# First attention of a two-layer decoder kernel: roots ahead of the weight blocks, weights cast one pair sooner

## The reference

```python
x = x + _L0_xattn_ref(_layernorm(x), ctx_1024, ctx_1024, mask)     # first attention, 16 batches
x = x + _L0_ffn_ref(_layernorm(x), ...)                            # 4 experts, 2 chosen for each batch by a gate
x = x + _L1_xattn_ref(_layernorm(x), ctx_1024, ctx_1024, ...)      # causal attention with 16 heads
x = x + _L1_ffn_ref(_layernorm(x), ...)                            # shared and chosen experts
```

## Time and profile before

| | us |
|---|---|
| median of 3 runs | 785.7 (784.28 to 785.91) |
| the profiled execution | 787.21 |
| its span | 785.4 |
| VectorE busy in the span | 621.0 |
| TensorE busy in the span | 717.4 |
| the gate's last products end | 90.4 after the start of the span |

### The profile page before, as it was taken

One profiled execution on the slowest core, in us unless ns is written; L12 is line 12 of the kernel. 1 busy time (PEld: TensorE's weight loads), 2 busy tenths in 40 slices (PEclk: granted clock), 3 DMA queues, 4 the chain that ended last, 5 costly groups with the idle time before them and its releaser, 6 DMA issues.

```text
span 785.4 us, 29153 instructions
## 1 busy us (share of the span) xinstructions
PE 717.4 (91%) x11006; PEld 571.9 (73%) x11006; DVE 621.0 (79%) x1803; ACT 337.8 (43%) x711; POOL 381.0 (49%) x647
## 2 busy tenths in 40 slices
PE   5688759999999999999999999999989999997896
PEld 5566547888888888888888888888766666665684
DVE  4777655788888887978787878788889988997864
ACT  4665423434343434343434344443455555553310
POOL 1788833354454445453535353544434544546354
PEclk9886689999999999999999999999999999999798
DMA  8776600000000000000000000000122222322120
GB/s 289 235 235 221 208 1 3 3 3 3 3 3 3 3 3 3 3 3 3 3 3 3 3 4 3 3 10 16 35 64 69 88 83 83 115 89 69 34 76 7
DMA packets 24655, 40.98 MB, mean 52 GB/s; under 512 B 3855, under 2 KB 16793, under 8 KB 24267
## 3 DMA queue, kind: packets, MB, share of 16 engines
q1 hardware_dynamic: 23096, 37.13, 14.4%
q0 software_dynamic: 704, 1.71, 0.8%
q10 hardware_dynamic: 726, 0.30, 0.2%
HBM read 30.60 MB, written 8.91 MB: 50 GB/s over the span
## 4 chain that ended last, share of the span: by engine, by line
PE 70%; DVE 15%; issue 5%; POOL 5%; ACT 4%; DMA 0%; POOLq 0%; ACTq 0%; DVEq 0%
PE ps L490 7%; PE ps L484 7%; PE ps L492 6%; PE ps L491 6%; PE ps L687 6%; DVE mx L1499 5%; PE ps L629 4%; PE ps L705 4%; PE ps L743 4%; PE ps L745 4%; PE ps L744 3%; PE ps L631 3%; PE ps L630 2%; PE ps L741 2%; PE ps L621 2%
## 5 line engine op out<-in xcount | busy, mean ns | idle before, releaser
L1113 ACT ACTIVATE pT<-ps 128x1024 f32<-128x1024 f32 x96 | 93.1, 1021 | 123.7 <-PE ps L687 123.7
L1499 DVE TENSOR_REDUCE mx<-ps 128x16 f32<-128x2048 f32 x48 | 109.5, 2281 | 1.0 <-PE ps L648 1.0
L2049 POOL TENSOR_TENSOR y<-y,vec 128x256 f32<-128x256 f32 x32 | 23.2, 724 | 170.7 <-DVE y L1270 170.7
L743 PE MATMUL ps<-xh,w_hi 128*128 128x128 bf16 x512 | 99.4, 219 | 0.0
L744 PE MATMUL ps<-xl,w_hi 128*128 128x128 bf16 x512 | 99.3, 219 | 0.0
L745 PE MATMUL ps<-xh,w_lo 128*128 128x128 bf16 x512 | 99.2, 219 | 0.0
L1959 POOL TENSOR_TENSOR rs<-rs,cst 128x1 f32<-128x1 f32 x132 | 75.6, 573 | 10.3
L1957 POOL TENSOR_TENSOR rs<-mv,cst 128x1 f32<-128x1 f32 x132 | 29.7, 225 | 102.2 <-DVE mv L1267 96.1
L490 PE MATMUL ps<-w_hi,hh 128*128 x256 | 69.8, 273 | 0.0
L491 PE MATMUL ps<-w_hi,hl 128*128 x256 | 69.8, 273 | 0.0
L492 PE MATMUL ps<-w_lo,hh 128*128 x256 | 69.8, 273 | 0.0
(11 more groups left out here) (355 smaller groups left out, 2462.9 us busy)
## 6 DMA issues: line engine op xcount, KB each, us to landing
stage<-in_w SPq DMA_DIRECT2D x32, 384.0 KB, 3.7
vec<-in_vec SPq DMA_DIRECT2D x4, 896.0 KB, 5.8
vec<-in_tw SPq DMA_DIRECT2D x12, 256.0 KB, 3.0
ctxc<-in_ctx SPq DMA_DIRECT2D x19, 128.0 KB, 2.3
comb<-x SPq DMA_DIRECT2D x16, 128.0 KB, 1.7
comb<-x1b SPq DMA_DIRECT2D x16, 128.0 KB
out<-x SPq DMA_DIRECT2D x16, 128.0 KB, 2.1
ytok<-t SPq DMA_DIRECT2D x14, 128.0 KB, 1.8
```

What stands on the lines that cost most here:

```text
L743: mm(dst, w(w_hi, c, j), xh[:, c, :], start=False, stop=False)
L1113: A(pT[:, 8 * a:8 * a + 8, :].rearrange("p h q -> p (h q)"), ps[:, 2 * a:2 * a + 2, :].rearrange("p g k -> p (g k)"), ACT.Exp, scale=SCALE ...
L1499: nc.vector.tensor_reduce(mx[:, :], att.rearrange("p g s k -> p (g s) k"), AX.X, ALU.max, negate=True).then_inc(m_max, 1)
```

## The change

- On POOL the roots of pair i+2 stand ahead of the weight block of pair i+1, and one add and one power of four columns serve the statistics of pair i+2 and the gate's of pair i-1; for the last three pairs the gate's roots stand alone. The tiles mv and rs have 8 places instead of 6.
- ACT casts three quarters of pair 0 ahead of the first exponentials, and in pair i the quarters of pair i+1, in the order 0, 2, 3, 1. POOL and the refills follow the same order. VectorE subtracts its quarter of pair i ahead of the reciprocals of the sums.
- The third pair of x is a transfer of its own, ahead of weight quarter 3. SP's wait for the cast of the constants stands ahead of the second pair's refills and bias rows, no longer ahead of the first's. The context of pair i+3 is loaded behind the four quarters.
- ACT's wait for wc_lo stands at the first encoder exponentials.
- Eight filling products stand ahead of the first shift's transpose.

```diff
@@ names
-        mv = sb("mv", [128, 6, 2])
-        rs = sb("rs", [128, 6, 1])
+        mv = sb("mv", [128, 8, 2])
+        rs = sb("rs", [128, 8, 1])
+        ORDER = (0, 2, 3, 1)
+        x_third = c_ctx
+        LAST_GATES = {PAIRS - 3: 4, PAIRS - 2: 8, PAIRS - 1: 16}
+
+        def pair_slot(i):
+            return 4 * (i % 2)
+
+        def gate_slot(i):
+            return 4 * ((i + 1) % 2) + 2
@@ block.sync
             sp.dma_start(stage[:, 2, :], w_d[:, 2 * QCH:3 * QCH]).then_inc(w_in[2], 16)
+            sp.dma_start(x[:, 4 * D:6 * D], x_d[:, 4 * D:6 * D]).then_inc(x_third, 16)
             sp.dma_start(stage[:, 3, :], w_d[:, 3 * QCH:4 * QCH]).then_inc(w_in[3], 16)
...
-            sp.dma_start(x[:, 4 * D:], x_d[:, 4 * D:]).then_inc(x_in2, 16)
+            sp.dma_start(x[:, 6 * D:], x_d[:, 6 * D:]).then_inc(x_in2, 16)
...
-            sp.wait_ge(cst_ready, 1)
...
             for i in range(PAIRS - 1):
+                if i == 1:
+                    sp.wait_ge(cst_ready, 1)
                 if i % 2 == 1:
                     bias_rows(i // 2)
-                next_quarter(i, 0)
-                next_quarter(i, 1)
+                for q in ORDER:
+                    next_quarter(i, q)
                 if i + 3 < PAIRS:
                     next_ctx(i, 0)
                     next_ctx(i, 1)
-                next_quarter(i, 2)
-                next_quarter(i, 3)
@@ block.tensor, gate_sums
-                    pe.wait_ge(a_grstd, n[j])
+                    if i in LAST_GATES:
+                        pe.wait_ge(a_grstd, LAST_GATES[i])
+                    else:
+                        pe.wait_ge(a_rstd, 2 * (i + 4))
@@ block.tensor, prep
-                    pe.wait_ge(c_ctx, (k - (B - 1)) * 16)
+                    pe.wait_ge(c_ctx, (k - (B - 2)) * 16)
@@ block.tensor, block
+                if n < 0:
+                    for _ in range(8):
+                        mm(ps[:, 5, :], identb[:, :],
+                           identb[:, :].rearrange("p (o k) -> p o k", o=1).broadcast_to([128, 4, 128]), start=True, stop=True)
                 shift_transpose(m)
@@ block.scalar
             mask_diagonals(1)
+            for q in ORDER[:3]:
+                weights_high(0, q)
             for i in range(PAIRS):
                 pair_exps(i)
...
-                weights_high(i, 0)
-                weights_high(i, 1)
-                weights_high(i, 2)
-                weights_high(i, 3)
+                if i == 0:
+                    weights_high(0, ORDER[3])
+                if i + 1 < PAIRS:
+                    for q in ORDER:
+                        weights_high(i + 1, q)
...
-            act.wait_ge(wc_ready, 1)
...
             def exps(u):
                 act.wait_ge(st_psum, u + 1)
+                if u == 0:
+                    act.wait_ge(wc_ready, 1)
@@ block.vector
             def weights_quarter(i):
-                dve.wait_ge(w_hi_ready, i * 4 + OWN + 1)
+                dve.wait_ge(w_hi_ready, i * 4 + ORDER.index(OWN) + 1)
...
                     gate_stats(i - 1)
-                pair_sums(i)
                 if i + 2 < PAIRS:
                     if i == 0:
+                        dve.wait_ge(x_third, 16)
+                    if i == 1:
                         dve.wait_ge(x_in2, 16)
                     pair_stats(i + 2)
-                if i + 1 < PAIRS:
-                    weights_quarter(i)
+                weights_quarter(i)
+                pair_sums(i)
...
-            dve.wait_ge(a_gveps, 2 * PAIRS - 4)
+            dve.wait_ge(a_gveps, LAST_GATES[PAIRS - 3])
             gate_stats(PAIRS - 1)
             gate_means(PAIRS - 3)
-            weights_quarter(PAIRS - 1)
@@ block.gpsimd
-            def pair_roots(i):
+            def pair_roots(i, with_gate):
+
                 pool.wait_ge(a_var, i * 2 + 2)
-                tt(rs[:, 0:2, :], mv[:, 0:2, 1:2], both(cst[:, C_EPS:C_EPS + 1]), ALU.add).then_inc(a_veps, 2)
+                n = 2
+                if with_gate:
+                    pool.wait_ge(a_gvar, (i - 3) * 2 + 2)
+                    n = 4
+                slots = slice(pair_slot(i), pair_slot(i) + n)
+                tt(rs[:, slots, :], mv[:, slots, 1:2], both(cst[:, C_EPS:C_EPS + 1], n), ALU.add).then_inc(a_veps, 2)
                 pool.wait_ge(a_veps, i * 2 + 2)
-                tt(rs[:, 0:2, :], rs[:, 0:2, :], both(halves), ALU.pow).then_inc(a_rstd, 2)
+                tt(rs[:, slots, :], rs[:, slots, :], both(halves, n), ALU.pow).then_inc(a_rstd, 2)
...
-            pair_roots(0)
-            pair_roots(1)
+            pair_roots(0, False)
+            pair_roots(1, False)
+            for q in ORDER[:3]:
+                weights_low(0, q)
             for i in range(PAIRS - 1):
-                weights_low(i, 0)
                 if i + 2 < PAIRS:
-                    pair_roots(i + 2)
-                weights_low(i, 2)
-                if i > 0:
+                    pair_roots(i + 2, i > 0)
+                else:
                     gate_roots(i - 1)
-                weights_low(i, 3)
+                for q in ORDER[:3]:
+                    weights_low(i + 1, q)
             gate_roots(PAIRS - 2)
             rstd(0, 1, y_var, y_veps, y_rstd)
             pool.wait_ge(a_gm, 2 * PAIRS - 4)
             gate_roots(PAIRS - 1)
-            weights_low(PAIRS - 1, 0)
-            weights_low(PAIRS - 1, 2)
-            weights_low(PAIRS - 1, 3)
```

More of the change, by code:

```diff
@@ L546, in gate_sums @@
                 n = counts(i)
-                slot = 2 + 2 * (i % 2)
+                slot = gate_slot(i)
                 for j in range(2):
-                    pe.wait_ge(a_grstd, n[j])
+                    if i in LAST_GATES:
+                        pe.wait_ge(a_grstd, LAST_GATES[i])
+                    else:
+                        pe.wait_ge(a_rstd, 2 * (i + 4))
                     xb = (i * 2 + j) * D
@@ L1286, in pair_stats @@
             def pair_stats(i):
+                slot = pair_slot(i)
                 for j in range(2):
-                    stats(tokens_of(i)[j], j, i * 2 + j, a_stats, a_var)
+                    nc.vector.memset(junk[:, 0:1], 0.0)
+                    nc.vector.bn_stats(st[:, j, :], tokens_of(i)[j]).then_inc(a_stats, 1)
+                    dve.wait_ge(a_stats, i * 2 + (j + 1))
+                    nc.vector.memset(junk[:, 1:2], 0.0)
+                    nc.vector.bn_aggr(mv[:, slot + j, :], st[:, j, :]).then_inc(a_var, 1)
             def pair_tokens(i):
@@ L1295, in pair_tokens @@
                         dve.wait_ge(a_T, i * 2 + (j - 1))
-                    normalized(ya[j][:, :], tokens_of(i)[j], j).then_inc(a_q, 1)
+                    normalized(ya[j][:, :], tokens_of(i)[j], pair_slot(i) + j).then_inc(a_q, 1)
             def masked_keys(c0, c1):
@@ L1961, in _, with both @@
             pool.wait_ge(cst_in, 16)
-            def both(col):
-                return col.rearrange("p (a o) -> p a o", o=1).broadcast_to([128, 2, 1])
-            def pair_roots(i):
+            def both(col, n):
+                return col.rearrange("p (a o) -> p a o", o=1).broadcast_to([128, n, 1])
+            def pair_roots(i, with_gate):
                 pool.wait_ge(a_var, i * 2 + 2)
-                tt(rs[:, 0:2, :], mv[:, 0:2, 1:2], both(cst[:, C_EPS:C_EPS + 1]), ALU.add).then_inc(a_veps, 2)
+                n = 2
[4 more added lines that the diff above has]
+                tt(rs[:, slots, :], mv[:, slots, 1:2], both(cst[:, C_EPS:C_EPS + 1], n), ALU.add).then_inc(a_veps, 2)
                 pool.wait_ge(a_veps, i * 2 + 2)
-                tt(rs[:, 0:2, :], rs[:, 0:2, :], both(halves), ALU.pow).then_inc(a_rstd, 2)
+                tt(rs[:, slots, :], rs[:, slots, :], both(halves, n), ALU.pow).then_inc(a_rstd, 2)
             def gate_roots(i):
                 pool.wait_ge(a_gvar, i * 2 + 2)
-                slot = 2 + 2 * (i % 2)
-                tt(rs[:, slot:slot + 2, :], mv[:, slot:slot + 2, 1:2], both(cst[:, C_EPS:C_EPS + 1]),
-                   ALU.add).then_inc(a_gveps, 2)
-                pool.wait_ge(a_gveps, i * 2 + 2)
-                tt(rs[:, slot:slot + 2, :], rs[:, slot:slot + 2, :], both(halves), ALU.pow).then_inc(a_grstd, 2)
+                slots = slice(gate_slot(i), gate_slot(i) + 2)
+                count = LAST_GATES[i] - LAST_GATES.get(i - 1, 0)
+                tt(rs[:, slots, :], mv[:, slots, 1:2], both(cst[:, C_EPS:C_EPS + 1], 2), ALU.add).then_inc(a_gveps, count)
+                pool.wait_ge(a_gveps, LAST_GATES[i])
+                tt(rs[:, slots, :], rs[:, slots, :], both(halves, 2), ALU.pow).then_inc(a_grstd, count)
             def weights_low(i, q):
-                pool.wait_ge(w_hi_ready, i * 4 + (q + 1))
+                pool.wait_ge(w_hi_ready, i * 4 + ORDER.index(q) + 1)
                 w0 = i * (4 * QCH) + q * QCH
```

## The result

The changed kernel takes 782.1 us (median of 14 runs, 779.55 to 785.0) beside 786.3 us for the kernel before on the same chip (14 runs, 784.28 to 787.91). The ratio is 0.9944, with a 95% interval from 0.9933 to 0.9956: 4.4 us less, where the forecast was 7.8 less.

The account below looks back on a forecast made before the run. Roots behind a weight block on POOL were taken to set the first attention's 9.7 us pair period. Stage -5.1, moved wait -0.7 and eight products -2.0 gave -7.8: 777.9 us against the median, range 773.5 to 784.3.

Parts of the forecast that it names:

- (b): First attention: refills take 4.6 instead of 3.4 us, 1.2 in each of three pairs; -4.2, 781.5 us; chance 0.12.
- (e): First attention: SP's wait ahead of the second pair's refills gives the weights' lead back; 781.1 us; chance 0.03.
- the 7.8: Whole change: the forecast's total gain in us, 777.9 us against the median; chance 0.45.
- the tail: From the last exponentials to the end of the gate's products: 11.2 us of sums, roots and small products, nothing gained.
- The moved wait: First projection: ACT no longer waits there for POOL's wc_lo, so VectorE's ql starts sooner; -0.7 us (0 to -1.0).
- The eight products: Ahead of the first shift's transpose: they keep TensorE at 2.4 GHz behind it; -2.0 us.
- a power of four columns: POOL's roots: extra cost over two columns lies between 0 and the whole saving; taken as 0.
- The stage: First attention, pair by pair: the last exponentials start at 74.1 instead of 79.24; -5.1 us.
- a ring: Pairs 5 to 7: one weight quarter's refill, cast, subtract and issue take 6.5 us, fitting in VectorE's 7.3 us period.
- Pair 2: First attention: bias rows land near 30.5, quarters at 31 to 34, exponentials start at 34.8; gain nothing.
- rival (c): First attention, slower: TensorE at 1.2 GHz needs 10.5 us a pair; 791.8 us (chance 0.05) or 784.3 us (0.12).
- a rule: Pair 2's transfers: at about 358 GB/s its 2.5 MB take 1.1 us more, whole gain 6.7; set aside for 426.

Follow-up runs that it names:

- experiment 1: The changed kernel without the eight filling products ahead of the first shift: 782.4 us, ratio 0.9967 to the kernel before.
- experiment 2: The changed kernel with ACT's wait for wc_lo back at its old place, ahead of the first projection's copies: 783.0 us, ratio 0.9967 to the kernel before.
- Experiment 8: The changed kernel with SP's wait for the constants and the bias rows one pair later: 778.1 us, ratio 0.9899 to the kernel before.
- Experiment 3: The changed kernel with all bias rows, and SP's wait for the constants, behind the last refill: 775.9 us, ratio 0.9878 to the kernel before.
- Experiment 5: The kernel of Experiment 3 plus eight filling products ahead of the second shift: 775.8 us, ratio 0.9871 to the kernel before.
- 9: The kernel of Experiment 5 with fourteen instead of eight filling products ahead of the first shift: 775.3 us, ratio 0.9866 to the kernel before.
- 11: The kernel of Experiment 3 without the eight filling products ahead of the first shift: 778.6 us, ratio 0.9893 to the kernel before.
- Experiment 7: The kernel before with only the bias rows and SP's wait for the constants moved behind the load of wc: 785.8 us, ratio 0.9992.
- 4: The kernel before with only POOL's roots, still two operations each, moved ahead of the weight blocks: 785.4 us, ratio 0.9998.
- 6: The changed kernel with POOL's first weight quarter ahead of the roots again: 790.2 us, ratio 1.0055 to the kernel before.
- 10: The kernel of Experiment 3 with six instead of three filling products a pair in the stage: 777.3 us, ratio 0.9890 to the kernel before.
- 12: The changed kernel with six instead of three filling products a pair in the stage: 783.5 us, ratio 0.9967 to the kernel before.

## Why the prediction was right, and where its size was off

**The direction was right, and all three parts of the change act where the forecast said.** The size was not: the gain of 4.4 lies at the rivals (b), 4.2, and (e), 4.6, which had 0.12 and 0.03, and not at the 7.8 that had 0.45. It would be smaller still without 1.7 us in the tail that the forecast called unchanged; as far as the forecast goes, that part is luck. The moved wait was put at -0.7 and is worth 0.85 to 0.9. The eight products were put at -2.0. That is the whole change between the first two maxima, but leaving them out brings back only 1.2 of it, and in the time 1.8 with an interval that begins at nothing; their worth over many executions stays open. The clock is 1.00 behind the first shift. On POOL the roots start when the statistics end in the last three of five places, and a power of four columns takes 1.01 us where one of two takes 0.69. The sum took it as free; POOL had the room, as the 0.65 us of idle time ahead of the add shows.

**The stage was mis-sized: -3.1 for -5.1.** The last exponentials moved by 1.4 us, not 5.1. The starts of the exponentials, forecast and measured (experiments 1 and 2 run the same program in this stage):

| pair | forecast | changed kernel | experiment 1 | experiment 2 |
|---|---|---|---|---|
| 2 | 34.8 | 36.33 | 35.22 | 34.75 |
| 3 | 44.0 | 45.42 | 45.36 | 44.68 |
| 4 | 51.0 | 52.05 | 52.21 | 51.76 |
| 5 | 59.5 | 62.22 | 60.68 | 60.20 |
| 6 | 66.8 | 69.26 | 71.26 | 69.49 |
| 7 | 74.1 | 77.81 | 78.30 | 76.99 |

At pair 4 all three are about 1 us late; by pair 7 it is 2.9 to 4.2. So most of the miss lies in pairs 5 to 7.

- *Pairs 5 and 6.* This is the step that failed. The sum let VectorE's own program set the period, 7.3 us, with a ring of "refill 3.4, cast 0.8, subtract 1.8, issue 0.5: 6.5 us" that fits in it. The refills took 4.7 us (median; 5.2 and 4.7 in experiments 1 and 2), and the third set of rows was in flight, 7.0 us from issue at 57.3 to landing: 373 GB/s at a share of 0.98 in 60 to 63, with TensorE busy 0.37 of 3 us. The casts waited 1.31 and 2.23, and pair 5 came 1.7 us later than the 1 us of pair 4. In experiments 1 and 2 the same waits (2.39 and 2.04, the longest) hit pair 6 instead. This was rival (b), put at 1.2 us in each of three pairs.
- *Pair 2, 1.5 late in the changed kernel's execution.* The bias rows landed sooner than forecast (25.06 + 4.5 = 29.6, for "near 30.5"), but "the quarters, 0.39 MB each at the 426 GB/s of a full stretch, at 31 to 34" did not. They were issued from 25.43 on and took 5.3 to 7.8 us, so the first was there at 30.7 and the last near 35.5 (27.9 + 7.6). Here the queues moved 356 GB/s, the mean of the three rows below. For rows, quarters and two blocks of the context, 2.7 MB, that is, as an estimate, 7.6 us instead of 6.4. The delay is not the same each time: in experiments 1 and 2 the queues moved 353 and 373 GB/s in this stretch, the quarters took 5.3 to 6.0 us, and the pair was 0.4 late and on time. Experiment 8 moves the rows past these refills, and pair 2 comes at 32.98.
- *Pair 7, 1.3 more, in the changed kernel's execution alone.* TensorE is busy all of 63 to 75 at a clock of 0.58, and VectorE waits 2.53 us for it. That is rival (c) in small. But the clock doesn't set the stage: in experiment 1 it was 0.91 in the same stretch, with TensorE busy 7.60 of 12 us, and the last exponentials came at 78.30, no earlier:

```profile
63.00:75.00 12.00, 7.60 (x44) 5.92 (x44) 6.63 (x21) 7.03 (x15) 10.36 (x12) 0.91 0.71 224
```

Windows of after in the stretch behind the first bias rows:

```profile
27.00:29.00 2.00, 2.00 (x9) 1.66 (x9) 0.11 (x1) 0.57 (x2) 1.71 (x3) 0.50 0.99 349
29.00:31.00 2.00, 2.00 (x7) 1.18 (x6) 1.31 (x5) 0.28 (x1) 0.00 (x0) 0.50 0.96 333
31.00:33.00 2.00, 2.00 (x13) 1.53 (x12) 1.92 (x12) 0.56 (x1) 1.37 (x2) 0.71 1.03 387
```

The forecast had weighed a rule here and set it aside: the Trainium skill, "DMA: Bandwidth & Descriptors", section "Specifications", names about 358 GB/s as what the memory gives one core. The mean of the three rows, 356, agrees with it; the last of them, 387, and the 426 of before do not. A gain 1.1 us smaller, as that rule gave, would have been nearer.

Experiment 3 settles the main point. With the rows out of the way the exponentials come at 41.80, 49.09, 58.30, 65.43 and 73.16, a microsecond ahead of the forecast's 74.1 (73.2 to 73.9 in the four executions of this stage, experiments 3, 5, 9 and 11), and the time is 775.9. So the path was read rightly, and where the rows are away its period nearly holds (24.1 us from pair 4 to pair 7, for 23.1); what the forecast priced at next to nothing was its own sentence "SP's wait for the constants moves from ahead of all refills to ahead of the second pair's", with 0.9 MB behind it. Experiment 7 shows why the trace of before could not warn of it: the same rows cost nothing there, since the refills had slack.

**The tail was called unchanged and gave 1.7.** The gate's two products took 1.26 us and take 0.36 now: -0.9. Before, POOL's last weight block ran beside them, in this row of POOL's timeline before:

```profile
86.81 5.26 POOL L1984 TENSOR_TENSOR w_lo<-stage,w_hi 128x384 bf16<-128x384 f32 x6
```

After, POOL's last block ends at 80.98 and POOL is idle there. In the runs with the old order (4 and 7) the products take 1.26 and 1.27 us, in all others 0.36. The Trainium skill, "GPSIMD Engine Reference", section "1. Specifications", says that GpSimd shares its memory interfaces with VectorE and contends with VectorE instructions that have two inputs there; by that rule such a product is slower beside a POOL block, and the rows agree. The normalising of a pair behaves alike, which the forecast, with its 1.9 us, did not use: in the changed kernel it takes 0.73 us three times, each time with POOL idle (as at 65.15), and 1.63 to 1.93 us three times, each time beside a block; in the kernel before it is beside one all six times and takes 1.81 to 1.91. The other 0.8 us lie between the last exponentials and these products (9.9 us before, 9.1 after); what they are made of was not taken apart.

**What the sum lacked** is what comes back behind the second shift, 1.1 us: the forecast took the clock's gain as kept. Some 0.7 of it lies between the second and the third maxima. Experiment 5 holds the clock there, but its time can't be told from version 3's, so whether this costs anything over many executions is open.

**Rival (e)**, that SP's wait gives the lead back, was given 3 in 100 and 781.1 us. As a mechanism it deserved more: moving that wait and its rows by one pair (8) gives back 3.5 us, and leaving them to the end 5.2. Which share is the wait's and which the bytes' is not shown, since the two runs are not told apart.

## What to carry to other kernels

When a step is moved sooner, list what stands ahead of its transfers on the issuing queue, and price it by all the bytes in that line at the rate a mixed stretch sustains (353 to 373 GB/s over 6 us here), not at the fullest 2 us (426). Even that can be too little: the last quarter of pair 2 took 7.6 us. A transfer that costs nothing while the ring behind it has slack is the next bound once the slack is spent: the same rows cost 0 in the old order and 5 us in the new. And where two waits form one circle, test the halves: here the roots first alone gained nothing and the weights sooner alone lost 4.3 us, with the two other parts of the change in it; all together gained 4.4.

## What the runs showed of the hardware

**The same code gets either clock, and here it didn't matter.** Versions 3, 5 and 9, the kernels of those experiments, are the same up to the gate. In 60 to 66 us the granted clock was 0.55 in version 3 and 1.00 in the other two; their last exponentials start at 73.16, 73.86 and 73.67. The low one was first. The rows are of version 3, then version 5.

```profile
60.00:66.00 6.00, 6.00 (x26) 4.70 (x24) 4.88 (x14) 4.53 (x11) 5.62 (x7) 0.55 0.71 195
```
```profile
60.00:66.00 6.00, 4.75 (x32) 3.65 (x31) 4.47 (x8) 2.56 (x5) 5.86 (x8) 1.00 0.81 236
```

The Trainium skill, "TensorE: Matmul & The Clock Gate", section "Part 1: The HAM clock gate", says that the moment of the change varies from run to run. The two rows agree that it varies; here they differ over the whole of six microseconds.

**Filling products may make the clock likelier to hold, but not sure.** Eight kernels have exactly eight of them ahead of the same 1.7 to 1.8 us of idle time. Between the first and the second maxima the clock held in four profiles (the changed kernel and experiments 5, 6 and 10; the maxima stand 10.5 to 10.7 us apart) and fell in four (2, 3, 8 and 12; 11.5 to 11.9). With fourteen (9) it held. In the five kernels without them (before, 1, 4, 7 and 11), with 3.5 to 3.7 us of idle time, it always fell (11.9 to 12.7). With one profile each this suggests an effect and doesn't prove it.
